# A cross-attention and routed-expert kernel on one core: all weight copies moved behind the first routed rows, dense blocks regrouped, the last tile normalised earlier

## What is computed

```python
x = x + xattn(layernorm(x), ctx)          # first half, about 175 us
scores    = layernorm(x) @ wr + br        # (rows, 8)
expert_id = argmax(scores)                # one expert per row
h = gelu(layernorm(x) @ w1[e] + b1[e])    # 128 -> 512
y = h @ w2[e] + b2[e]                     # 512 -> 128
out = x + y[expert_id]
```

## Time and profile before

| | before |
|---|---|
| median of 3 runs | 232.77 us |
| profiled execution, its own time | 234.39 us |
| its span, first to last instruction | 232.7 us |
| mean granted TensorE clock | 0.944 |
| TensorE busy | 201.1 us (86%) |
| VectorE busy | 180.6 us (78%) |
| ScalarE busy | 157.9 us (68%) |
| GpSimd busy | 128.6 us (55%) |

### The profile page before, as it was taken

The page is one execution under the profiler, slowest core; times in us unless marked ns, Lnnn a source line. Parts: engine busy times, 40 slices in busy tenths (PEclk is TensorE's granted clock), DMA queues, the critical chain, the costliest instruction groups (busy, mean ns, idle before and its releaser), DMA issues.

```text
span 232.7 us, 5011 instructions
## 1 busy us (share of the span) xinstructions
PE 201.1 (86%) x1837; PEld 150.3 (65%) x1837; DVE 180.6 (78%) x395; ACT 157.9 (68%) x249; POOL 128.6 (55%) x177
## 2 busy tenths in 40 slices
PE   0379969999999999989989899899993797999980
PEld 0133417776766767757666566789973686899970
DVE  2899797697998998998995997958756435776872
ACT  2752899399399699699595799689531445667650
POOL 3695718807915807978508947744400740066763
PEclk9999985899999999999999999999996569999998
DMA  6999979899999999999999999988994369999200
GB/s 215 389 251 263 226 223 237 192 234 174 220 215 216 278 230 269 241 198 233 216 213 256 184 220 258 201 196 185 239 263 121 120 219 290 346 370 378 98 11 12
DMA packets 142958, 51.78 MB, mean 223 GB/s; under 512 B 121172, under 2 KB 140773, under 8 KB 142934
## 3 DMA queue, kind: packets, MB, share of 16 engines
q1 hardware_dynamic: 142000, 50.08, 93.2%
q0 software_dynamic: 784, 1.38, 1.7%
q10 hardware_dynamic: 150, 0.00, 0.0%
HBM read 10.74 MB, written 3.75 MB: 62 GB/s over the span
## 4 chain that ended last, share of the span: by engine, by line
PE 49%; DVE 21%; DMA 11%; issue 8%; ACT 4%; POOL 3%; SPq 2%; DVEq 0%; POOLq 0%
DMA PT<-Phl 10%; PE psX L1079 5%; PE psS L1061 5%; PE psO L1079 5%; PE psS L1060 5%; PE psS L1059 5%; DVE S L800 5%; DVE Phl L817 3%; PE psS L1290 3%; PE psX L1081 3%; PE psO L1081 3%; ACT S L651 3%; SPq L393 2%; PE psS L1276 2%; PE psS L1296 2%
## 5 line engine op out<-in xcount | busy, mean ns | idle before, releaser
L651 ACT ACTIVATE S<-S,negb 128x1024 f32<-128x1024 f32 x48 | 55.1, 1147 | 18.4 <-DVE negb L808 18.4
L800 DVE TENSOR_SCALAR_CACHE_REDUCE S<-psS 128x1024 f32<-128x1024 f32 x48 | 58.2, 1217 | 11.4 <-PE psS L1061 11.2
L817 DVE TENSOR_TENSOR Phl<-S,Phl 128x1024 f16<-128x1024 f32 x38 | 51.5, 1355 | 5.0 <-ACT Phl L666 4.8
L533 POOL TENSOR_TENSOR Phl<-S,Phl 128x256 f16<-128x256 f32 x40 | 26.3, 689 | 51.7 <-ACT Phl L666 51.7
L666 ACT CAST Phl<-S 128x1024 f16<-128x1024 f32 x48 | 50.3, 1047 | 5.2 <-DMA PT<-Phl 3.7
L1059 PE MATMUL psS<-qT,gh 128*128 128x512 f16 x96 | 37.7, 393 | 5.4 <-DVE S L800 2.6
L1079 PE MATMUL psX<-qn,PT 128*128 128x256 f16 x204 | 36.4, 273 | 2.1 <-DMA PT<-Phl 2.1
L1079 PE MATMUL psO<-qn,PT 128*128 128x256 f16 x204 | 37.3, 276 | 0.9 <-DMA PT<-Phl 0.8
L1061 PE MATMUL psS<-qT,gl 128*128 128x512 f16 x96 | 37.9, 395 | 0.0
L1060 PE MATMUL psS<-qT,gh 128*128 128x512 f16 x96 | 37.9, 394 | 0.0
L1081 PE MATMUL psO<-qn,PT 128*128 128x128 f16 x204 | 35.7, 221 | 0.0
(11 more groups left out here) (239 smaller groups left out, 425.3 us busy)
## 6 DMA issues: line engine op xcount, KB each, us to landing
PT<-wp SPq DMA_DIRECT2D x8, 512.0 KB, 6.0
stageT<-in_ctxT SPq DMA_DIRECT2D x6, 512.0 KB, 7.0
qn<-wp SPq DMA_DIRECT2D x6, 512.0 KB, 7.3
wp<-in_w SPq DMA_DIRECT2D x4, 512.0 KB, 4.9
stageT<-in_w SPq DMA_DIRECT2D x4, 512.0 KB, 4.9
rows_by_expert<-stageT SPq DMA_DIRECT2D x4, 385.5 KB, 5.6
PT<-Phl SPq DMA_TRANSPOSE x48, 4.2
S<-rows_by_expert SPq DMA_DIRECT2D x2, 258.0 KB, 5.4
```

The lines of the kernel that those rows point to most:

```text
L533: last = nc.gpsimd.tensor_tensor(lo[:, r], slot(t, e)[:, r], hi[:, r], ALU.subtract)
L651: nc.scalar.activation(slot(t, e), slot(t, e), ACT.Exp, bias=negb[:, t:t + 1], accum_out=Lp[:, t * NG + e:t * NG + e + 1]).then_inc(exp_do ...
L800: nc.vector.tensor_scalar(out=into, in0=bank(u, n)[:, 0:into.shape[1]], scalar1=1.0 / GS, scalar2=None, op0=ALU.mult, op1=ALU.max, accum_o ...
L817: nc.vector.tensor_tensor(lo, slot(t, e), hi, ALU.subtract).then_inc(low_done, 1)
```

## The change

Four things are edited. `DENSE_AT` goes from (0, 1, 2, 3, 4, 10, 16, 21) to (0, 1, 2, 3, 4, 5, 20, 21). SyncE's two fetches that stood ahead of the wait for `rows_sent` now stand behind the first and the second batch's read. The experts' registers are loaded at once. On VectorE the normalisation of tile 7 stands ahead of the positions, and the low part of tile 7 between the addition and the product of the ranks.

```diff
-    DENSE_AT = (0, 1, 2, 3, 4, 10, 16, 21)
+    DENSE_AT = (0, 1, 2, 3, 4, 5, 20, 21)
-    FIRST = 2
...
-            sp.reg_load(expert_reg[0:FIRST], bexp[0:1, 0:FIRST])
-            ex = [sp.snap(r, min_val=0, max_val=E - 1) for r in expert_reg[0:FIRST]]
+            sp.reg_load(expert_reg[0:NB], bexp[0:1, 0:NB])
+            ex = [sp.snap(r, min_val=0, max_val=E - 1) for r in expert_reg]
...
-            for b in range(FIRST):
-                fetch(b)
-            sp.reg_load(expert_reg[FIRST:NB], bexp[0:1, FIRST:NB])
-            ex += [sp.snap(r, min_val=0, max_val=E - 1) for r in expert_reg[FIRST:NB]]
             sp.wait_ge(rows_sent, 16 * TA)
             block_rows(0, 0, D, rows_landed)
+            fetch(0)
             block_rows(1, 0, D, rows_landed)
+            fetch(1)
             fetch(2)
             block_rows(0, D, ROW, rest_landed)
...
             statistics(x1, TA, T)
+            normalise(x1, x2n, TA, T, x2n_ready)
...
             link(nc.vector.tensor_tensor(rank[:, :, :], rank_psum.rearrange("p (t e) -> p t e", e=E),
                                          sblk[:, :].unsqueeze(1).broadcast_to([P, TA, E]), ALU.add))
+            dve.wait_ge(x7T_high, 1)
+            nc.vector.tensor_tensor(xTp[:, 1, NB, :], x7T_psum, xTp[:, 0, NB, :], ALU.subtract).then_inc(x7T_low, 1)
             link(nc.vector.tensor_tensor(rank[:, :, :], rank[:, :, :], oneh[:, :, :], ALU.mult))
             link(nc.vector.tensor_reduce(out=posf[:, :], in_=rank[:, :, :], axis=AX.X, op=ALU.add))
             nc.vector.tensor_copy(pos[:, :], posf[:, :]).then_inc(pos_ready, 1)
-
-            normalise(x1, x2n, TA, T, x2n_ready)
...
-            dve.wait_ge(x7T_high, 1)
-            nc.vector.tensor_tensor(xTp[:, 1, NB, :], x7T_psum, xTp[:, 0, NB, :], ALU.subtract).then_inc(x7T_low, 1)
```

## The result

The changed kernel takes **237.88 us**, the median of 4 runs (237.16 to 238.28), where the kernel before takes 232.91 us (4 runs, 232.75 to 233.84): a ratio of 1.0171, with an interval of 1.0132 to 1.0211, 5.0 us slower. The forecast was 236.0 with a range of 234.2 to 239.2. The profiled execution of after took 238.28 us, with a span of 236.6 us and a mean clock of 0.946.

What follows compares the result with a forecast made beforehand. Full DMA engines, a little ahead of a full TensorE, were taken to bound the second half. turn(2) +3.5 us and the end -0.4 gave +3.1: from the median 232.77 to 235.9, called 236.0 us, range 234.2 to 239.2.

Steps and rivals of the forecast that it cites:

- The sum: Whole kernel: +3.5 us at turn(2) less 0.4 at the end, +3.1 us; bounds +1.4 to +4.4.
- rival 1: TensorE's new waits halve its clock, ahead of batch 0's split (hidden) or of turn(2) (2.7 us more, 238.7); chance 0.27.
- Part one: VectorE's new order: dense blocks start 1.60 us earlier, positions are ready 1.85 us later.
- Part two: GpSimd's sends and batch 0's read come 1.7 us later, the read at 192.8; loading 14 registers is free.
- Part three: SyncE's full queue: two copies add 2.8 us, a departing instruction fetch saves 0.4; turn(2) starts 3.5 us later.
- Part four: Behind turn(2): the work is the same and TensorE full, so the shift stays; later copies have cover.
- Part five: Program end: GpSimd's last transfer leaves the end, the dense result is last; gain 0 to 0.8 us, taken as 0.4.
- Rival 2: DMA queue has room for both copies, batch 2 lands by 204.6 or so; 0.5 to 1 us faster, 232.1; chance 0.08.
- Rival 3: Copies and reads partly overlap or land in another order; turn(2) moves 1 to 2 us, 233.9 to 234.4; chance 0.08.

Runs made afterwards that it cites:

- e1: Changed kernel with fetch(0) and fetch(1) put back ahead of the wait for the rows; ratio 1.0061 to the kernel before.
- e3: Changed kernel once more, unchanged, for a second profile; ratio 1.0134 to the kernel before.
- e4: Changed kernel with batch 2's read moved ahead of fetch(4) and fetch(5) in SyncE's queue; ratio 1.0106 to the kernel before.
- e10: Changed kernel with the grouping of dense blocks undone, moved copies and VectorE's new order kept; ratio 1.0136 to the kernel before.
- e11: Changed kernel with only half of every weight copy made, the first layer's weights; ratio 0.9925 to the kernel before.
- e6: Kernel before with VectorE's new order alone; four runs, median 237.6 us against 235.26 us, too wide for an interval.
- e5: Kernel before once more, unchanged, for a second profile; ratio 0.9952.
- e7: Kernel before with the new grouping of dense blocks alone (six first, two last); ratio 0.9967.
- e12: Kernel before with only the dense block at place 16 moved to place 20, timed a second time; ratio 0.9928, 232.2 to 234.46 us.
- e2: Kernel before with both copies moved behind the first reads and the registers loaded at once, nothing else; ratio 1.0088.
- e8: Changed kernel with VectorE's order undone, moved copies and new grouping kept; ratio 1.0056 to the kernel before.
- e9: Kernel before with only the dense block at place 16 moved to place 20, first timing; ratio 0.9853.

## Why the prediction was right, and where not

The forecast, slower by the two copies in the full queue, holds, and the measured time lies in its range. The sum, +3.1, was 1.8 too small against the 4.9 of the second half. It was also beyond the sum's own bounds: they end at +4.4, 237.2 us, and 237.88 lies in the range only because the range was widened to 239.2 for rival 1, the clock, which is not what made the difference at turn(2). That part of being right is luck. By its steps:

**Part one** held to 0.01 us: dense blocks 1.60 us earlier (5.17 to 3.57, relative), positions ready 1.85 us later (2.15 to 4.00).

**Part two** is the step that was mis-sized, on one side of a pair. The last send ended 1.64 us later (relative 12.25 to 13.89), near the 1.7 that were forecast. But SyncE's read then waited 3.27 us behind it, in place of 1.64. The trace counts the landing of the 16 shares of a transfer one by one: in after 15 shares of the last send were there by 191.56 and the sixteenth at 193.34. Meanwhile an instruction fetch ran, from 190.52 to 192.09. The first piece below is this fetch, one packet, by the DMA queues of 190.50 to 190.54 (245.2% of 16 engines over 0.04 us are 1.57 us on one); the second is all that began on the engines from 192.10 to 193.34.

```profile
q8 instruction: 1, 0.02, 245.2%
```

```profile
q0 software_dynamic: 2, 0.00, 1.5%
```

For 1.2 us the engines began nothing but two small packets, and SyncE stood waiting; this is its list of waits from 170 to 215 in after, and behind it the same in e1, where SyncE comes to the wait later, as it loads registers twice:

```profile
SPq L448 <- DMA rows_by_expert<-qT,S: 8.2, 1, 8.2
```

```profile
SPq L449 <- DMA rows_by_expert<-qT,S: 3.7, 1, 3.7
```

It is the same fetch that I had seen in the earlier trace rows inside the queue of reads, and whose departure I priced in part three. The runs show it as a pattern. In the six in which it began within 0.45 us of the end of the last send (after, e1, e3, e4, e10, e11), the last share landed 1.18 to 1.26 us behind the end of the fetch, and 1.05 to 1.78 us behind the fifteenth. In the other eight, where it began 2.1 us or more after that end, the last two shares lie at most 0.10 us apart. e6 is one of these: its last send ends 1.44 us later than before's, the instruction fetch begins 2.14 us behind that end, and SyncE's read stands 1.61 us behind it, as in before. That the fetch and the late share were on the same DMA engine is not in the records; it is argued from these fourteen runs. The Trainium skill, "DMA: Bandwidth & Descriptors", section "Why a DMA increments its semaphore by 16 and not by 1", says that a transfer's engines finish independently and that only the full count means that all of it has landed. The trace agrees: 15 of 16 at 191.56, and nobody could go on until 193.34.

**Part three.** Two copies were priced at 2.8 us, and the instruction fetch was taken off with 0.4 of a possible 1.5. The runs show that the two prices hang on each other. From batch 0's read to batch 2's landing it takes:

| | instruction fetch among the reads | instruction fetch ahead of the reads |
|---|---|---|
| copies ahead of the wait | 12.71 to 13.36 (before, e5, e6, e7, e12) | 11.57 (e1) |
| copies behind the reads | 14.93 (e2), 15.03 (e8) | 14.48 (after), 14.45 (e3), 14.35 (e10) |

So two copies cost 2.8 to 2.9 us with the instruction fetch outside the queue and 1.6 to 2.3 us with it inside, and its leaving gave 1.1 to 1.8 us in the queue of before and only 0.5 to 0.7 in that of after. The fetch did leave the queue as the prediction allowed, and what it gave back there, and more, it took ahead of batch 0's read. I had written the gain of its leaving and not asked where it would go: 15.3 us forecast from batch 0's read to batch 2's landing, 14.48 measured, and 17.16 for the read in place of 15.6. Together turn(2) moved by 4.29, where 3.5 was forecast and 4.4 was the upper bound. e4 and e8 confirm the place: with two copies fewer ahead of batch 2's read the wait is gone, and with the sends on time it is longer (1.50 us). "Over 2 us" of idle time ahead of turn(2) were forecast; it was 0.96, since TensorE waited ahead of turn(0) and came later.

**Part four** failed in its cover. That the copies have room holds for the later ones and not for the first. TensorE's list of waits from 180 to 234 names no copy of weights; these are its long ones:

```profile
PE psS L1292 <- DVE Phl L981: 2.7, 4, 1.5
PE psX L1241 <- DMA S<-rows_by_expert: 2.5, 2, 1.6
PE psS L1272 <- DVE S L973: 1.9, 2, 1.6
```

But the list puts a wait down to one engine where it may have had more to wait for. The last line has the wait of 1.59 us ahead of the first sent `up`, at 198.05 (TensorE's timeline, at the top). VectorE's step for batch 0 ended at 197.57; fetch(0), issued at 193.87, took 4.1 us and landed its last share at 197.96. VectorE's timeline of after, and its DMA issues of 193.8 to 194.0:

```profile
197.01 0.56 DVE L973 TENSOR_TENSOR S<-psX,S 128x384 f16<-128x384 f32 x1 [1.42 <-ACT S L697]
```

```profile
PT<-wp SPq DMA_DIRECT2D x1, 512.0 KB, 4.1
```

In after, e3, e4 and e10 the first sent `up` starts 0.49 to 0.53 us behind VectorE's step, in e2 0.98 us, and in each 0.09 us behind the last share of fetch(0); in the other nine profiles it starts 0.06 us behind VectorE's step. So the moved copy itself holds TensorE for 0.4 us in after, a wait that the prediction did not count; there it is hidden, as TensorE waits again at turn(2).

Behind turn(2) another 1.93 us are lost, for which the prediction had no term. (e5, the kernel of before, needs 24.73 us from turn(2) to the last block's result, where before had 23.85, so about half of this is within what two profiles of one kernel differ by.) They are where VectorE waits for a result of TensorE. Its waits in after from 207.9 to 233.7, and in before from 204.6 to 228.5:

```profile
DVE stageT L991 <- PE psS L1292: 7.2, 6, 2.2
```

```profile
DVE stageT L995 <- PE psS L1296: 4.4, 7, 1.0
```

Two results come about 1 us late. VectorE's timeline of after shows the first, and TensorE's that, by its records, the product had ended by 217.02:

```profile
217.84 0.29 DVE L991 TENSOR_TENSOR stageT<-psS,S 128x128 f32<-128x128 f32 x1 [1.73 <-PE psS L1292]
...
230.03 0.29 DVE L991 TENSOR_TENSOR stageT<-psS,S 128x128 f32<-128x128 f32 x1 [1.57 <-PE psS L1292]
```

```profile
216.63 0.39 PE L1292 MATMUL psS<-qn,Phl 128*128 128x128 f16 x4
...
218.79 0.40 PE L1292 MATMUL psS<-qn,Phl 128*128 128x128 f16 x4 [0.39 <-DVE Phl L981]
```

Blocks follow each other at VectorE every 1.6 us; these two took 2.82 and 2.66. Steps of 2.5 us or more behind turn(2), apart from the one that has the wait at turn(2) in it, stand in after, e1 to e4, e7, e8 and e10 (one or two in each), once in e5 (2.58), and not in before, e6, e9, e11 and e12. So they go mostly with the copies behind the reads or with 14 sent blocks in a row, and with the bytes of the copies (e11); e5 has one with neither. **What causes them stays open**: the ends of TensorE's matmuls are modelled, instruction fetches lie near but not at them, and no run took one suspect away alone.

**Part five** had a gain, for the wrong reason. The gain is 1.30 us, not 0.4, and GpSimd's last transfer is still what ends the span, not the dense result. In before, after and all twelve runs the span ends 3.33 to 3.35 us after that transfer has left GpSimd: 1.12 to 1.14 us until it has landed, 0.18 us, then a drain of GpSimd's of 1.79 us, and 0.23 us to the end. The drain is in the trace of both kernels at the line that opens the program:

```profile
L82 POOLq DRAIN  x1: 1790/1790/1790, 230.6 to 230.6; - x1
```

```profile
L81 POOLq DRAIN  x1: 1790/1790/1790, 234.5 to 234.5; - x1
```

I had compared when the two transfers land (dense: 230.05 before, 235.25 after) and not what GpSimd does behind that. Two dense blocks at the end are 2.5 us behind the last sent result, too few to take 5.4 us of transfer, landing and drain off the path; by 1.3 us they shorten it.

**The rivals.** Rival 1, the clock: it did fall, from 197.50 to 200.91, behind the waits for batch 0, the first of the two places named. turn(1) took 1.06 us, where e5 has 0.61. There it was hidden, as the rival said: TensorE still arrived 0.96 us early at turn(2). Behind turn(2) the clock was 1.00 (stretch from 207.90). Not hidden it would be where TensorE is late itself, in e4, e6 and e10, which have no wait at turn(2). Rival 2 (the copies fit) is refuted by e1 and e2. Rival 3 (half paid) describes e8, not after.

By the times the two terms, late sends and late copies, each cost about half and add up within the intervals: 1.0056 (1.0010 to 1.0103) without the order, 1.0061 (1.0012 to 1.0110) without the copies' move, 1.0134 to 1.0171 with both. At turn(2) they do more than add: it comes 0.72 us later than before in e1, 1.42 in e8, and 4.29 in after (3.70 in e3). With late sends alone, the 0.59 us of slack and the shorter queue took up most of the 2.5 us by which batch 0's read was late. What e1's profile loses beside that lies behind turn(2), where its two late results are.

## What to carry to other kernels

A transfer that stands ahead of a wait is paid for by a resource that is idle; moved behind the wait into a queue that is full, it costs a large part or all of its time (1.6 to 2.9 us for two copies), and the reader finds this by the DMA share of the two stretches. Where a list puts a wait down to one engine, compare the time at which that engine was done: 0.4 us of the wait ahead of the first sent `up` were a copy's. When a term of the sum is "this delay may go away", ask where it goes: the instruction fetch left the reads, and where it went the last send landed late. At the end of a program, count what an engine does after its last transfer has landed, not the landing alone; moving one dense block to the end gained 0.7% here.

## What the runs showed of the hardware

- An instruction fetch of 16 KB is one packet, 0.92 to 1.86 us long at this place of the program in the fourteen profiles; in the six in which an indirect transfer in 16 shares was issued just ahead of it, the sixteenth share landed 1.05 to 1.78 us behind the fifteenth.
- Behind its last indirect transfer GpSimd has 1.12 to 1.14 us to the landing and a drain of 1.79 us; the span ended 3.33 to 3.35 us after the transfer in all fourteen profiles.
- A load of 14 registers took 3.56 us where the DMA engines stood at a share of 0.21; one of 12, behind two copies of weights, took 4.88 us.
- The unchanged first half ends between 175.18 and 177.22 us in the fourteen profiles (0.06 and 0.74 us apart in two pairs of the same kernel), so that places in the second half had to be compared from a common point.
